# Shared expert's down product as three fp32r terms, with its rows held in twelve places and the first expert weights moved

## The reference, cut to what matters

```python
logits = x_flat @ gate_w.T                       # 8 experts
scores = softmax(logits); _, topk_ids = top_k(scores, 2)
gu = einsum('nh,eih->nei', x_flat, experts_gate_up)    # 2 x 352 per expert
h = silu(g) * u
expert_out = einsum('nei,ehi->neh', h, experts_down)
out = einsum('neh,ne->nh', expert_out, w)
shared = silu(x_flat @ shared_gate_w.T) * (x_flat @ shared_up_w.T) @ shared_down_w.T   # 704 wide
shared_weight = sigmoid(x_flat @ shared_expert_gate_w.T)
out = out + shared_weight * shared
```

## Time and profile before

| | |
|---|---|
| median of 3 runs | 479.7 us (478.91 to 481.79) |
| profiled execution | 479.78 us, its span 478.1 us |
| PE busy | 462.0 us, 97% of the span |
| DVE, ACT, POOL busy | 287.1, 201.8, 242.8 us |
| shared expert's steps and routing on PE | 94.7 to 213.4 us |
| expert blocks on PE | 213.4 to 355.3 us |
| second layer | from 355.3 us |

### The profile page before, as it was taken

The page is one execution under the profiler, slowest core; times in us unless marked ns, Lnnn a source line. Parts: engine busy times, 40 slices in busy tenths (PEclk is TensorE's granted clock), DMA queues, the critical chain, the costliest instruction groups (busy, mean ns, idle before and its releaser), DMA issues.

```text
span 478.1 us, 9570 instructions
## 1 busy us (share of the span) xinstructions
PE 462.0 (97%) x3166; PEld 382.7 (80%) x3166; DVE 287.1 (60%) x651; ACT 201.8 (42%) x452; POOL 242.8 (51%) x324
## 2 busy tenths in 40 slices
PE   7999999999999999999999999999998899999996
PEld 6777767687777788779999999999987667767685
DVE  5879986562353122335455545545556779999895
ACT  3555775477620022003332332233232555676752
POOL 6323443155337557267895553233231665766654
PEclk9999999999999999999999999999999999999999
DMA  8999600020002223999913333222116400000104
GB/s 275 388 411 353 96 13 1 1 88 2 0 1 93 85 70 107 309 281 218 314 38 110 101 100 89 70 68 76 47 39 203 158 1 2 2 2 0 45 14 165
DMA packets 48144, 53.00 MB, mean 111 GB/s; under 512 B 15425, under 2 KB 42370, under 8 KB 47842
## 3 DMA queue, kind: packets, MB, share of 16 engines
q1 hardware_dynamic: 38562, 29.51, 22.0%
q0 software_dynamic: 7664, 20.19, 12.7%
q10 hardware_dynamic: 1872, 2.69, 1.8%
HBM read 35.25 MB, written 17.12 MB: 110 GB/s over the span
## 4 chain that ended last, share of the span: by engine, by line
PE 83%; DVE 6%; ACT 4%; issue 2%; DMA 2%; POOL 0%; SPq 0%; ACTq 0%; POOLq 0%; DVEq 0%
PE banks L1263 12%; PE banks L1316 10%; PE banks L347 6%; PE banks L1367 6%; PE banks L325 5%; PE banks L1368 5%; PE banks L1371 5%; PE banks L361 5%; PE banks L314 4%; PE banks L336 3%; PE banks L1389 3%; PE banks L1390 3%; PE banks L1393 3%; PE banks L1379 3%; PE banks L978 2%
## 5 line engine op out<-in xcount | busy, mean ns | idle before, releaser
L1201 ACT ACTIVATE hg<-banks 128x352 f32<-128x352 f32 x39 | 18.1, 465 | 98.4 <-PE banks L1371 98.4
L115 POOL TENSOR_TENSOR rstd<-var,mhalf 128x2 f32<-128x2 f32 x30 | 20.8, 695 | 74.7 <-DVE var L108 74.7
L1541 DVE TENSOR_TENSOR hgT_lo<-banks,hgT_hi 128x256 fp32r<-128x256 f32 x78 | 24.1, 350 | 56.3 <-ACT hgT_hi L1208 56.3
L1367 PE MATMUL banks<-w_hi,xgT_hi 128*128 x156 | 54.7, 351 | 0.1
L515 DVE TENSOR_REDUCE mx<-banks 128x16 f32<-128x1024 f32 x32 | 39.1, 1221 | 20.9 <-PE banks L325 20.7
L1368 PE MATMUL banks<-wd,xgT_hi 128*128 x156 | 50.3, 323 | 0.0
L1316 PE MATMUL banks<-sdn,big 128*128 128x256 f32 x192 | 47.5, 393 | 0.0
L1316 PEld LDWEIGHTS banks<-sdn,big 128*128 128x128 f32 x192 | 34.1, 189 | 12.6 <-issue 9.0
L1098 POOL DMA_INDIRECT expert_rows_in<-xn,slot x32 | 31.4, 980 | 18.4 <-issue 6.7
L325 PE MATMUL banks<-kvb,qT 64*128 64x256 f32 x256 | 36.3, 401 | 2.2 <-DVE pw L518 0.9
L1371 PE MATMUL banks<-w_hi,xgT_lo 128*128 x156 | 37.6, 322 | 0.0
(11 more groups left out here) (250 smaller groups left out, 1163.8 us busy)
## 6 DMA issues: line engine op xcount, KB each, us to landing
w_hi<-in_egu POOLq DMA_DIRECT2D x2, 2816.0 KB, 21.6
expert_rows_in<-zeros SPq DMA_DIRECT2D x1, 5304.0 KB, 40.9
xn<-expert_rows_in SPq DMA_DIRECT2D x39, 128.0 KB, 2.1
y_all<-choices_out SPq DMA_DIRECT2D x16, 256.0 KB, 5.2
wd<-in_egu SPq DMA_DIRECT2D x4, 704.0 KB, 7.2
out_x<-x SPq DMA_DIRECT2D x7, 256.0 KB, 2.3
x<-in_x SPq DMA_DIRECT2D x2, 768.0 KB, 7.4
wd<-in_edown POOLq DMA_DIRECT2D x4, 384.0 KB, 6.6
```

The costliest lines, as they stand in the source:

```text
L1367: nc.tensor.matmul(to, xgT_hi[:, c, k, :], hi, start=(k == 0), stop=False)
```

## The change

It does four things.

1. **Three terms.** `down(g)` works in fp32r with split operands. ACT rounds `sdn` to `sdn_hi` (`round_shared_down`, two instructions, 1280 and 256 columns), DVE makes `sdn_lo` (`split_shared_down`, two instructions). The hidden values are split too: DVE multiplies for all n (`hidden`, now into `act_s`), ACT writes the high part (`high_part(n)`, one place behind `silu(n + 1)`), and the low part is made by POOL for n < 12 and by DVE from 12 on (`low_part`). Each row tile has 18 matmuls of 256 columns where it had 6 fp32 ones. `copy_up` is gone.
2. **Twelve places.** The 24 high and low parts go round in twelve places (`HELD_IN`), six where `hT` was, four over `xn2T`, two over `xT` and `qT`; `sdn_hi` lies over the attention weights. So high_part(n) waits for down(0) from n = 8 and for down(1) from n = 16.
3. **Order.** down(0) stands before up(8), `rank_choices` behind up(8). The pace of the scattering is written anew for that order.
4. **Expert weights.** ACT loads only expert 0. SP waits for the end of down(3) (`d_ready` 16) before it loads expert 1, waits for the landing of that one's down weights, and goes on with 2 and 3, 4, 5, and 6 and 7, with the fetches between them; then come the second layer's four attention weight matrices, which were loaded at 102 us before, and only then fetch(9). POOL makes the low parts of expert 1, and loads the high down weights of experts 1 to 4 only after the end of down(3).

```diff
-            load_d(act, 0, 2, 1, d_in)
-            load_w(act, 1, 2, w_in[1])
+            load_d(act, 0, 1, 1, d_in)
...
             sp.wait_ge(scattered, 16 * 2 * NT)
             for b in range(NX):
                 fetch(sp, b)
+            sp.wait_ge(d_ready, 16)
             sp.wait_ge(d_in, 16 * KI)
-            sp.wait_ge(w_in[1], 16 * KD)
+            load_w(sp, 1, 2, w_in[1])
+            load_d(sp, 1, 2, 1, d_in)
+            for b in range(NX, NX + 2):
+                fetch(sp, b)
+            sp.wait_ge(d_in, 32 * KI)
             load_w(sp, 2, 4, w_in[2])
             load_d(sp, 2, 4, 1, d_in)
-            for b in range(NX, NX + 3):
-                fetch(sp, b)
-            sp.wait_ge(h2_done, 2 * KS)
-            sp.wait_ge(ranked, 1)
+            fetch(sp, NX + 2)
             load_w(sp, 4, 5, w_in[3])
             load_d(sp, 4, 5, 1, w_in[3])
             fetch(sp, NX + 3)
             load_w(sp, 5, 6, w_in[4])
             load_d(sp, 5, 6, 1, w_in[4])
             fetch(sp, NX + 4)
-            sp.wait_ge(d_ready, 16)
             load_w(sp, 6, E, w_in[5])
             load_d(sp, 6, E, 1, w_in[5])
+            for dst, src in ((wk, wk1), (wv, wv1), (wq[1], wq1), (wo[1], wo1)):
+                sp.dma_start(dst[:, :, :], split(src)).then_inc(attn1_in, 16)
             for b in range(NX + 5, NB):
                 fetch(sp, b)
...
-            for n in range(2 * KS):
-                hidden(n)
+            for n in range(NH):
+                low_part(n)
                 if n + 5 < NU:
                     rstd2(n + 5)
...
             pool.wait_ge(g_ready, 4 * KS)
             pool.wait_ge(h2_done, 2 * KS)
-            load_d(pool, 0, 2, 0, d_hi_in[0])
+            load_d(pool, 0, 1, 0, d_hi_in[0])
             pool.wait_ge(d_hi_in[0], 16 * KI)
+            pool.wait_ge(d_ready, 16)
+            load_d(pool, 1, 5, 0, d_hi_in[0])
+            pool.wait_ge(w_hi_in, 16 * KD)
+            pool.wait_ge(lo_made, 1)
             pool.wait_ge(w_in[1], 16 * KD)
-            load_d(pool, 2, 5, 0, d_hi_in[0])
-            pool.wait_ge(w_hi_in, 16 * KD)
+            make_w_lo(nc.gpsimd, 1)
...
+            def high_part(n):
+
+                rows = slice(0, SR[n % KS])
+                if n == 1:
+                    wait(act, events["wo_ready"], NU)
+                if n >= 8:
+                    wait(act, d_ready, 8 if n >= 16 else 4)
+                wait(act, t_done, n + 1)
+                nc.scalar.activation(h_part(n, 0)[rows, :], act_s[rows, n % FACTORS, :], ACT.Copy).then_inc(hi_done, 1)
...
             def down(g, between=None):
-                if g < 2:
-                    wait(pe, h_done, KS * g + KS)
-                else:
-                    wait(pe, h2_done, KS * (g - 2) + KS)
+                pe.wait_ge(sdn_ready, 4)
+                wait_low_part(pe, KS * g + KS - 1)
+                terms = [(x, w, j) for j in range(KS) for x, w in ((0, sdn_hi), (0, sdn_lo), (1, sdn_hi))]
                 for c in range(2):
                     wait(pe, sh_added, 4 * g + 2 * c - 2)
                     for t in range(2):
-                        for j in range(KS):
+                        for m, (x, w, j) in enumerate(terms):
                             last = nc.tensor.matmul(psum[4 + c][:, t * D:(t + 1) * D],
-                                                    hT[0:SR[j], (g + 1) % 2, j, (2 * c + t) * P:(2 * c + t + 1) * P],
-                                                    sdn[0:SR[j], j, :], start=(j == 0), stop=(j == KS - 1))
+                                                    h_part(KS * g + j, x)[0:SR[j], (2 * c + t) * P:(2 * c + t + 1) * P],
+                                                    w[0:SR[j], j, :], start=(m == 0), stop=(m == len(terms) - 1))
                         last.then_inc(d_ready, 1)
...
-            for n in range(2, 2 * KS):
+            for n in range(2, 8):
                 up(n)
...
-            down(0, (0, rank_choices))
-            for n in range(2 * KS, 2 * KS + 2):
+            down(0)
+            up(8)
+            rank_choices()
+            for n in range(9, 2 * KS + 2):
                 up(n)
             down(1)
...
+            add(0)
+            hidden(8)
             dve.wait_ge(ranked, 1)
...
             link(v.tensor_tensor(hot["slots"][:, :, :], rank, inc[:, :, :].rearrange("p e t -> p t e"), ALU.add))
+            hidden(9)
...
+            for n in range(10, 4 * KS):
                 hidden(n)
-            add(1)
-            for n in range(2 * KS + 2, 4 * KS):
-                hidden(n)
+                if n - 1 >= NH:
+                    low_part(n - 1)
+                if n == 2 * KS + 1:
+                    add(1)
+            low_part(4 * KS - 1)
             dve.wait_ge(w_hi_in, 16 * KD)
             dve.wait_ge(w_in[0], 16 * KD)
             make_w_lo(v, 0)
             add(2)
-            dve.wait_ge(w_in[1], 16 * KD)
-            make_w_lo(v, 1)
```

More of the change, by code:

```diff
@@ L898, in factor_rows, with h_part, wait_low_part @@
         def factor_rows(n):
-            return HIGH if n >= NH and n % KS == KS - 1 else slice(0, SR[n % KS])
+            return HIGH if n % KS == KS - 1 else slice(0, SR[n % KS])
         def ups(n):
             return n - n // KS
-        act_s, up_s = mem["pw"][:, 0:3, :], mem["pw"][:, 2:4, :]
-        hT = big[:, 0:2 * KS * SG].rearrange("p (b j n) -> p b j n", b=2, j=KS)
+        act_s = mem["pw"]
+        FACTORS = 4
+        HELD_IN = [0, 1, 2, 3, 4, 5, 6, 7, 0, 1, 2, 3, 4, 5, 8, 9, 6, 7, 0, 1, 2, 3, 10, 11]
+        def h_part(n, lo):
+            at = HELD_IN[n]
+            if at < KS:
+                return (hT_lo if lo else hT_hi)[:, at, :]
+            if at < KS + 4:
+                return (xn2T_lo if lo else xn2T_hi)[(at - KS) // 2][:, (at - KS) % 2, :]
+            return hT_more[:, at - KS - 4, lo, :]
+        def wait_low_part(engine, n):
+            if n < NH:
+                wait(engine, h_done, n + 1)
+            else:
+                wait(engine, h2_done, n - NH + 1)
         xg = mem["xn"][:, :, :, :].rearrange("p b t n -> p (b t) n")
@@ L1076, in gpsimd_on @@
                                          if s is g_ready or u % KS < KS - 1]
-            downs = lambda first, end: [(d_ready, n, 11) for n in range(first, end)]
-            products = downs(1, 5) + halves(2 * KS, 2 * KS + 2) + downs(5, 9) + halves(2 * KS + 2, 4 * KS - 2)
+            downs = lambda first, end: [(d_ready, n, 10) for n in range(first, end)]
+            products = halves(2 * KS - 1, 2 * KS + 2) + downs(5, 9) + halves(2 * KS + 2, 4 * KS - 1)
             length = sum(w for _, _, w in products)
@@ L1188, in scalar_on @@
                     keep_logits(LOGITS_AT[n])
+                if n == 4:
+                    round_shared_down()
                 if n == max(TURNED_AT):
@@ L1193, in scalar_on @@
                     nc.scalar.activation(col["sg"][:, :], lg[:, :, E], ACT.Exp, scale=-1.0).then_inc(ex_done, 1)
-            for n in range(2 * KS, 4 * KS):
-                silu(n)
+            high_part(4 * KS - 1)
             def silu_rows(b):
@@ L1247, in up @@
                 wait(nc.tensor, silu_done, n - 1)
-                wait(nc.tensor, u_copied, n - 1)
+                wait(nc.tensor, t_done, n - 1)
             elif n == NH + 2:
@@ L1434, in split_transposed, with hidden, split_shared_down @@
                                     xn2T_hi[n // 2][:, :, at].bitcast(F32), ALU.subtract).then_inc(xL_ready, 1)
+        def hidden(n):
+            bank, rows = up_at(n)
+            wait(nc.vector, silu_done, n + 1)
+            wait(nc.vector, u_ready, ups(n + 1))
+            nc.vector.tensor_tensor(act_s[0:SR[n % KS], n % FACTORS, :], bank[rows, :], act_s[rows, n % FACTORS, :],
+                                    ALU.mult).then_inc(t_done, 1)
+        def split_shared_down():
+            nc.vector.wait_ge(sdn_ready, 2)
+            for rows, ks in ((slice(0, P), slice(0, KS - 1)), (slice(0, SR[5]), slice(KS - 1, KS))):
+                nc.vector.tensor_tensor(sdn_lo[rows, ks, :], sdn[rows, ks, :], sdn_hi[rows, ks, :].bitcast(F32),
+                                        ALU.subtract).then_inc(sdn_ready, 1)
         def vector_on():
@@ L1439, in vector_on @@
             n = 0
+            hidden(1)
             stats2(5)
             stats2(6)
-            for u in range(3, NU):
+            split_transposed(3)
+            stats2(7)
+            for u in range(4, NU):
+                hidden(u - 2)
                 split_transposed(u)
-                if u == 3:
-                    stats2(7)
+            split_shared_down()
+            hidden(6)
+            hidden(7)
             def link(ins):
```

74 lines of the change are left out of this document (36 added, 38 removed).

## The result

The changed kernel takes 489.4 us (median, 488.6 to 490.1) against 480.25 us beside it: ratio 1.0189, 95% interval 1.0151 to 1.0227, or 9.1 us slower. The forecast was 484.0 us, the range 472 to 490 holds the measurement. The profiled execution took 488.6 us, its span is 486.9.

What follows compares the result with a forecast made beforehand. PE was taken to bound the kernel. 479.8 - 5.4 (down products' saving left after the scattering wait) + 7.9 (expert weights and queue of loads) + 1.6 (clock) = 483.9, say 484.0 us; own range 481 to 487, wide range 472 to 490.

Steps and rivals of the forecast that it cites:

- What bounds it, and that waits take the lead back: Whole kernel: PE, busy 97% of the span, sets the time; new waits consume what its quicker down products save.
- Three terms: Shared expert's down products in fp32r: 8.65 us each instead of 11.73; four save 12.4 us if nothing else is late.
- Rival (d): Shared down product: fp32r misses 0.12 us per matmul because two of three terms load new rows; +2 us; chance 0.05.
- The first wait: First transposes, inside down(3): PE waits 5.5 us for scattered rows until 203.3; 7.0 of the 12.4 us are lost.
- Rival (b): Scattering doesn't hold PE: first fetch lands before 198, all 12.4 us come through, 471 us; chance 0.13.
- the prediction's own signs of being wrong: No wait at the transposes, fetch(9) landing by 32 us after down(3), or a wait in a place passed over.
- The second wait: Third expert block: PE waits 3.2 us (bounds 1.5 and 5) for expert 1's weights, loaded and split after down(3).
- The third wait: Ninth block: fetch(9), behind 9.1 MB at 325 GB/s, lands 37 us after down(3); +7.9 us, including the second wait.
- my slow bound: Ninth block's fetch: the queue of loads moves at only 300 GB/s, costing +10.3 us instead of +7.9.
- The rival of fast loads: Queue before the ninth block: loads are fast enough, from 380 GB/s up, so no wait; 479 us; chance 0.20.
- The clock: After PE's waits the clock may halve: 1.0 us at the first wait plus 0.6 at the last, 1.6 in all.
- Rival (c): After waits: clock stays low long, 4.3 + 3.6 us instead of 1.6, queue at 300 GB/s; 492.6 us; chance 0.15.

Runs made afterwards that it cites:

- the product without 64 rows: The changed kernel with the shared down product's 64-row matmuls replaced by 128-row ones, same count and columns: 493.8 us, ratio 1.0253, in the series with gaps in PE's work.
- the products' reversal: The changed kernel, PE's waits on expert weights' low parts against constants, with every second row tile of a shared down product in reverse term order: 486.8 us, ratio 1.0149.
- the earlier scattering: The changed kernel with fetches before loads, expert 1's down weights first, alternate tiles reversed, plus low parts 10 and 11 moved from POOL to DVE: 473.6 us, ratio 0.9883.
- expert 1's weights first: The changed kernel, PE's low-part waits against constants, with POOL loading and splitting expert 1's down weights before loading those of experts 2 to 4: 489.3 us, ratio 1.0207.

## Why the prediction was right and wrong

**What bounds it, and that waits take the lead back: right.** Order and places hold: PE ends the shared expert earlier, loses it at expert 1 and at fetch(9), and ends later than before.

**Three terms: wrong, and it didn't matter.** The step was "a down of 72 costs 8.65", from the experts' down product at 0.12. Measured 9.94 to 10.14, because of the seven changes of row count; about 7 us were saved instead of 12.4. Rival (d) said that the product would miss 0.12 because of new rows at every term; it does miss it, but the product without 64 rows shows that this is not why. The experts' product has 128 and 96 rows, and their steps show no such cost, so the nearest row was the wrong neighbour. The 11.73 us of before contained the same changes, unseen in a mean of 0.244.

**The first wait: absent, with its end in place.** Predicted: PE at the transposes 5.5 us early, held until 203.3, E = 208.0. Measured: PE gets there by itself at 203.1, E = 208.4. The slower product used up just the time that the wait would have taken; that E came out within 0.4 us is the floor where that wait ends, and luck in that PE reached it just then. Rival (b) wanted the first fetch landed before 198; it is issued only at 199.69. A missing wait at the transposes stands among the prediction's own signs of being wrong. Scattering started at 152.99 (predicted 150.9) and was through near 199.7 (200.3). That the floor exists, the products' reversal and the earlier scattering show.

**The second wait: split.** 3.2 us were predicted ahead of the third block; 1.7 came there: the gate and up weights landed by 212.65, after 4.3 us instead of 5.5, and the block started at E + 7.6 instead of E + 9.2 (the terms written down, 5.5 and 3.17, add up to 8.7). The other 2.3 came at the fourth, for the low part of expert 1's down weights, which the prediction does not mention. The row is POOL's load, issued at 208.90, whose 1.4 MB landed 12 us after the end of its issue, beside SP's. As predicted, the third wait takes both in; expert 1's weights first gave nothing by itself.

**The third wait: the step that failed, in its size.** "28 us, so fetch(9) lands at E + 37": it landed at E + 41.8, 4.8 later, beyond even my slow bound of E + 39.4. The queue's start was right (E + 9, 217.4). In the 32.8 us until the landing 10.14 MB moved, where I had counted 9.1: 8.57 on SP's queue (8.05 counted; among the rest are fetches 10 to 12, 0.4 MB, issued behind the ninth) and 1.53 on POOL's (1.08 counted; 0.44 are the rest of its first load, which landed at 222.4). 1.04 MB at my 325 GB/s are 3.2 us. The rate was 309: 10.14 MB at 309 instead of 325 are 1.6 us more. Together 4.8. This split holds by construction, since the rate is bytes by time; no run tests it apart. What the runs show is the cause as a whole: the same bytes in another order bring block 9's transposes to E + 32.4. The rival of fast loads, which wanted E + 32 with the order as it was, is refuted; the sum from the Trainium skill that it cites is given, in that section, for DMAs that GpSimd issues, and the queue here is SP's. The Trainium skill's page "DMA: Bandwidth & Descriptors", section "Where 436 GB/s comes from", says that transfers between HBM and SBUF are bounded by some 358 GB/s instead. By this estimate 10.14 MB take 28.3 us; measured were 32.8. The best stretch of before, 386, lies above that bound, so the measurement does not agree with it either.

**The clock: nearly.** 1.6 us predicted, 1.0 of it at the first wait, which did not come; 2.3 measured, all at block 9. Rival (c), 4.3 + 3.6, was too much. The half clock behind the fourth block's wait (226 to 228) disappears in the wait that follows.

**The sum.** Predicted −5.4 + 7.9 + 1.6 = +4.1 against the profiled execution of before. Measured −5.1 at E, +12.7 until block 9's transposes, +2.3 for the clock: +9.9, of which the last microseconds of the kernel gave 1 back. The middle term, 4.8 us short, is most of the difference of 5.8; the clock is 0.7 and E 0.3.

## What to carry to other kernels

When loads are moved behind an event, add up every byte ahead of the first small transfer that an engine needs, the other queues' too, and put small urgent transfers ahead of large patient ones: here that order alone was worth 10 us. A wait in front of a longer wait that has its own clock costs nothing, and removing it gains nothing, until the longer one is gone; so remove the last one first. Take a matmul's step from a row with the same row counts, and look where the count changes.

## What the hardware showed that I had not expected

- A change between matmuls of 128 and of 64 contraction rows costs PE 0.19 us here, in fp32r and, by 0.59 us for three changes, in fp32. Between 128 and 96 rows the timeline shows nothing of the kind. The Trainium skill's "TensorE: Matmul & The Clock Gate", section "Why this matters for your kernels", says that a matmul on 32 rows takes as long as one on 128; the trace agrees for 64 behind 64 rows (0.12), and adds the price of the change.
- The issue of a DMA has no fixed length: one L981 row of three DMAs took SP 3.61 us at 230.98, against 1.44 at 209.21. I read this as a queue that is full and holds its issuer; the profile does not show how full it is.
- The granted clock was half (1.2 GHz) behind waits of 6.8, 2.3 and 2.7 us, from 250.2 to about 255 and from 224.8 to about 228 in the changed kernel, and full (2.4 GHz) behind one of 2.1 us and behind 1.6 us after idle matmuls.
- In one series the kernel before took its usual time and the variants were some 10 us slower, with PE idle for nothing that the profile names; the same kernels on a chip of the same number had none of this later.
